# Decoder layer on one core: pair loops written out, and a broadcast by one fp32 matmul split into two fp32r matmuls

## The chip, the core and the metric

The kernel runs on one NeuronCore of one Trainium2 chip. The metric is the device time of one execution in microseconds (us); a kernel's time is the median of its runs. PE is the matmul engine (PEld its weight loads), DVE the vector engine, ACT the scalar engine, POOL GpSimd, SP the queue that issues the DMA transfers. "fp32r" is a four-byte type in which PE multiplies in one pass; an fp32 matmul shows two records in the trace. Wherever the kernel wants more than the precision of fp32r it splits a value into a rounded high part and the low remainder (`_hi`, `_lo`).

## The reference, cut to what matters

```python
x = x + attn(_layernorm(x))      # 32 heads of 128, q and k RMS-normed over all 4096 columns
x = x + xattn(_layernorm(x))     # quantised x @ quantised context
x = x + ffn(_layernorm(x))       # base linear + 8 low-rank experts weighted by a router

# inside attn, x is (2, 256, 512):
q = x @ Wq + bq;  k = x @ Wk + bk;  v = x @ Wv + bv        # each (2, 256, 4096)
k = gk * k * rsqrt(mean(k * k, axis=-1) + 1e-6)             # q likewise
attn = softmax(einsum('bhqd,bhkd->bhqk', q, k) / sqrt(128))
out = einsum('bhqk,bhkd->bhqd', attn, v) ... @ Wo + bo
```

The key norm that the change touches is `rsqrt(mean(k*k))`: one number per token, 512 tokens. Keys lie transposed (a head's 128 columns on the partitions, tokens along the row), so the 512 numbers are needed on every partition.

## The kernel before

All is on one core; each engine has its own program, written out by hand, and semaphores order them. There is no planner.

**k and q stage.** `project` (L540) makes one head's k (then q) for all 512 tokens: 12 matmuls of 128x512, three for each of four chunks of the model width (high by high, low by high, high by low), L549 to L551. "Unit" u counts them: 0 to 31 for k, 32 to 63 for q. ACT casts the weights to `w_hi` (L785) and takes the result out of PSUM (L799, L800: the square), DVE makes `w_lo` (L1205), POOL adds the squares up (L1056, into `acc_k`, then `acc_q`). `project` waits for `w_lo_dve`, so for DVE's L1205 of its own unit; weights and PSUM results have two buffers each. SP loads raw weights four units ahead and waits for the same semaphore.

**The key norm.** In the first four q units PE sums `acc_k` over partitions (L558), DVE scales it (L1282), POOL takes the power -1/2 (`rk_t`, L1064). DVE makes four diagonal matrices, `diag[:, t, :] = ident * rk_t[:, t]` (L1291), and then the weights' low part of q unit 4 (L1205). PE multiplies a matrix of ones by `diag` (L582), which puts every token's factor on all partitions; DVE copies it to `rkb` (L1294) and works the 32 heads of `k_all` through L1210 (a scalar_tensor_tensor of three operands in SBUF), spread over the q units that follow. On PE the L582 matmul stands between q unit 3 and q unit 4.

**Pair stage.** 16 pairs of heads, four slots each (head by batch). In a slot PE does, for successive slots, `scores`, four transposes of the probabilities (L612), 12 matmuls for v of the next pair, six of the output projection and six of probabilities by v. ACT, DVE and POOL have a `pair` of their own with the slot's casts, softmax and low parts. Pair 0 is written out, pairs 1 to 10 are a hardware loop of five turns (`Fori`, two pairs each), pairs 11 to 14 are written out, pair 15 has its own code. SP's `pair_loads` has a loop for pairs 1 to 7. Inside a loop the numbers that a semaphore is waited for depend on the turn and come from registers.

**Tail.** Cross attention, router and FFN follow, straight code on all engines.

Of the kernel before, what the change touches and what calls it, by code (L numbers as in the profile page):

```python
# [19 lines left out]
F32 = mybir.dt.float32  # L20
# [7 lines left out]
P = 128  # L28
B, S, D = 2, 256, 512
T = B * S  # L30
NT = T // P
# [18 lines left out]
def decoder_layer(nc, x, ctx_t, wk, wq, wv, wo, bk, bq, bv, bo, gk, gq, qscal, ra_w, base_b, router_b, bm_w,  # L50
                  expert_map, out):
    st = ExitStack()
    with st:
        def sem(name):
            return st.enter_context(nc.semaphore(name))
# [18 lines left out]
        def here(name, shape, dt, at=None):  # L74
            return place(name, shape, dt, at)[0]
# [21 lines left out]
        ident = here("ident", [P, P], F32)  # L97
        ident_r = here("ident_r", [P, P], F32R)
        ones = here("ones", [P, P], F32)
        bk_c = here("bk_c", [P, NH], F32)  # L100
        bq_c = here("bq_c", [P, NH], F32)
        bv_c = here("bv_c", [P, NH], F32)
# [20 lines left out]
        acc_k = here("acc_k", [P, T], F32, vh_at + half)  # L123
        acc_q = here("acc_q", [P, T], F32, vh_at + half + 2048)
        rkb = here("rkb", [P, T], F32, vl_at + half)
        diag = here("diag", [P, NT, P], F32, vl_at + half + 2048)
        square = here("square", [P, 2, T], F32, pt_at)

        xin = here("xin", [P, NT, D], F32, q_at + (NH - NT) * T * 4)
# [88 lines left out]
        ssq_out = sem("ssq_out")  # L218
        rms_done = sem("rms_done")
        diag_made = sem("diag_made")  # L220
        rkb_ready = sem("rkb_ready")
        k_normed = sem("k_normed")
        kq_hi = sem("kq_hi")
# [112 lines left out]
        @block.sync  # L336
        def _(sp):
            for t in range(NT):
                sp.dma_start(xin[:, t, :], x[t]).then_inc(x_landed[t], 16)
            for r in range(4):  # L340
                sp.dma_start(raw[:, r, :], wk[r]).then_inc(w_landed[r], 16)
            for dst, src in ((bk_c, bk), (bq_c, bq), (bv_c, bv), (g_c, gk), (gq_c, gq)):
                sp.dma_start(dst[:], src).then_inc(const_landed, 16)

            def load_heads(w, i, before):

                for r in range(4):
                    sp.wait_ge(w_lo_dve, before + 4 * i + r - 3)
                    sp.dma_start(raw[:, r, :], w[bass.ds(4 * i + r, 1)].rearrange("a p n -> (a p) n")
                                 ).then_inc(w_landed[r], 16)  # L350

            sp.dma_start(qs_b[:], qscal.partition_broadcast(P)).then_inc(qs_landed, 16)
            for i in range(1, NH // 4):
                load_heads(wk, i, 0)
                if i <= NT:
                    g = slice(2 * (i - 1), 2 * i)
                    sp.dma_start(ctx_f[:, g, :], ctx_t[:, g, :]).then_inc(ctx_landed[i - 1], 16)
                if i == NT:
                    sp.dma_start(bo_b[:], bo.partition_broadcast(P)).then_inc(x_bo_landed, 16)
                    for t in range(NT):  # L360
                        sp.dma_start(xb[:, t, :], x[t]).then_inc(x_bo_landed, 16)
            sp.wait_ge(ctx_quantised, B * NC // 2)
            sp.dma_start(ctx_kept, ctx_k[:]).then_inc(ctx_kept_out, 16)
            with sp.Fori(0, NH // 4) as i:
                load_heads(wq, i, NH)

            def load_wv(pair, c, n):
                sp.dma_start(raw[:, n, :], wv[bass.ds(2 * pair + c, 1)].rearrange("a p n -> (a p) n")
                             ).then_inc(w_landed[n], 16)

            def load_wo(h):
                sp.dma_start(raw[:, 1, :], wo[bass.ds(h, 1)].rearrange("a p n -> (a p) n")
                             ).then_inc(w_landed[1], 16)

            for n in range(4):

                sp.wait_ge(w_lo_dve, U1 - 3 + n if n < 2 else U1 + n - 1)
                load_wv(n // 2, n % 2, n % 2)

            def pair_loads(p):  # L380
                for j in range(3 if peeled(p, NP - 1, NP) else 4):
                    if peeled(p, 0, 1) and j < 2:
                        sp.wait_ge(w_lo_dve, U1 + 3 + j)
                    else:
                        sp.wait_ge(w_lo_pool, 4 * p + j - 1 + peeled(p, NP - 1, NP) * (j // 2))
                    if j % 2:
                        load_wo(2 * p + j // 2)
                    else:
                        load_wv(p + 2, j // 2, 0)

            pair_loads(0)
            with sp.Fori(1, 8) as p:
                pair_loads(p)

            pair_loads(8)
            pair_loads(9)
            sp.wait_ge(scores_ready, 2 * 18)
            pair_loads(10)
            sp.dma_start(wo_last_f[:], wo[NH - 1]).then_inc(wo_last_landed, 16)
            sp.dma_start(ra_f[:], ra_w).then_inc(ra_landed, 16)  # L400
            sp.dma_start(bm_f[:], bm_w).then_inc(bm_landed, 16)
            sp.dma_start(bb_b[:], base_b.partition_broadcast(P)).then_inc(base_b_landed, 16)
            sp.dma_start(rb_b[:], router_b.partition_broadcast(P)).then_inc(router_b_landed, 16)
            sp.dma_start(em_i[:], expert_map.partition_broadcast(P)).then_inc(map_landed, 16)
            pair_loads(11)
            sp.wait_ge(scores_ready, 2 * 22)
            sp.wait_ge(ctx_kept_out, 16)
            sp.dma_start(ctx_q[:], ctx_kept).then_inc(ctx_back, 16)
            for p in range(12, NP - 1):
                pair_loads(p)  # L410
            pair_loads(NP - 1)
            for n, (t, cols, y) in enumerate(out_parts()):
                sp.wait_ge(out_done, n + 1)
                sp.dma_start(out[t][:, cols], xn[:, t, cols]).then_inc(stored, 16)
            sp.wait_ge(stored, 16 * (NT + 1))
# [89 lines left out]
        def _(pe):  # L505
# [62 lines left out]
            for r in range(4):  # L568
                pe.wait_ge(xb_lo_done, r + 1)
                for part in (xb_hi, xb_lo):  # L570
# [7 lines left out]
            sum_squares(acc_k, p_flat[0], NH)  # L578
            project(0, 2, NH)
            project(0, 3, NH)  # L580
            pe.wait_ge(diag_made, NT)
            pe.matmul(p_flat[1], ones[:], diag[:].rearrange("p t n -> p (t n)"), start=True, stop=True  # L582
                      ).then_inc(rkb_ready, 1)
            with pe.Fori(1, NH // 4) as i:
                for r in range(4):
# [90 lines left out]
            def pair(p, par, first=False):  # L676

                for j in range(4):
                    b = j % 2
                    h = 2 * p + j // 2  # L680
                    s = 2 * h + b
                    scores(h + b, 1 - b)
                    transpose_probs(s, b)
                    if first:
                        v_tile(p + 1, j, 1 - par, w_lo_dve, U1 + 4)
                    elif peeled(s, NS - 5, NS - 4):
                        v_tile(p + 1, j, 1 - par, w_lo_pool, 4 * p - 1, range(0, NC - 1))
                    else:
                        v_tile(p + 1, j, 1 - par, w_lo_pool, 4 * p - 1)
                    if not (first and j < 2):  # L690
                        project_out(h - 1, b)
                    if j == 0:
                        pe.wait_ge(v_lo_done, 2 * p + 2)
                    probs_v(s, j // 2, b, par, b)
# [29 lines left out]
            v_tile(0, 3, 0, w_lo_dve, U1 + 2)  # L724
            pe.wait_ge(ssq_out, 2)
            pair(0, 0, first=True)
            with pe.Fori(0, (NP - 6) // 2) as i:
                pair(2 * i + 1, 1)
                pair(2 * i + 2, 0)
            for p in range(NP - 5, NP - 1):  # L730
                pair(p, p % 2)
            last_pair()
# [45 lines left out]
        def _(act):  # L778
# [24 lines left out]

            act.wait_ge(consts_made, 1)
            act.copy(ident_r[:], ident[:])

            def normalise_x(t):
                act.wait_ge(ln_shift, t // 2 + 1)
# [155 lines left out]
                last_out_hi(3)  # L964

            pair(0, 0)
            with act.Fori(0, (NP - 6) // 2) as i:
                pair(2 * i + 1, 1)
                pair(2 * i + 2, 0)
            for p in range(NP - 5, NP - 1):  # L970
                pair(p, p % 2)
            last_pair()
# [63 lines left out]
        def _(pool):  # L1036
# [61 lines left out]
            def pair(p, par):  # L1098
                for j in range(4):
                    h = 2 * p + j // 2  # L1100
                    if j % 2 == 0:
                        split_kq_lo(h + 1)
                        pair_chunk_lo(par, j // 2, 0, 4 + 4 * p + j)
                    else:
                        chunk_lo(wo_lo[:], wo_hi[:], 1, 4 + 4 * p + j)
                    if peeled(p, NP - 5, NP - 4) and j == 0:
                        pool.memset(ones_b[:], 1.0).then_inc(ones_b_made, 1)
# [5 lines left out]
                pair_chunk_lo(1, 1, 0, n + 2)  # L1113

            pair(0, 0)
            with pool.Fori(0, (NP - 6) // 2) as i:
                pair(2 * i + 1, 1)
                pair(2 * i + 2, 0)
            for p in range(NP - 5, NP - 1):
                pair(p, p % 2)  # L1120
            last_pair()
# [17 lines left out]
        def _(dve):  # L1139
# [148 lines left out]
            weights_lo(0, 3, NH)  # L1288
            dve.wait_ge(rms_done, 1)
            for t in range(NT):  # L1290
                dve.tensor_scalar(diag[:, t, :], ident[:], rk_t[:, t:t + 1], None, ALU.mult).then_inc(diag_made, 1)  # L1291
            weights_lo(1, 0, NH)
            dve.wait_ge(rkb_ready, 1)
            link(dve.tensor_copy(rkb[:], p_flat[1]))  # L1294
# [102 lines left out]
                        late_lo((s - 49) // 2)  # L1397

            pair(0, 0)
            with dve.Fori(0, (NP - 6) // 2) as i:  # L1400
                pair(2 * i + 1, 1)
                pair(2 * i + 2, 0)

            for p in range(NP - 5, NP - 1):
                pair(p, p % 2)
# [237 lines left out]
```

## Time and profile before

| | |
|---|---|
| time, median of 3 runs | 532.8 us (531.97 to 533.22) |
| the profiled execution's own time | 531.9 us |
| its span (first to last instruction) | 530.1 us |
| PE busy | 519.8 us, 98% |
| DVE, ACT, POOL busy | 333.8, 355.2, 264.3 us |
| granted TensorE clock | 1.00 |
| k and q stage, about | 9 to 186 us |
| pair stage, about | 186 to 495 us |

The span is what the trace covers; 1.8 us of the profiled time lie around it. Matmul records overlap each other (a 128x512 fp32r matmul shows 0.39 us, but its successor starts 0.23 us after it), so places in PE's stream are read from starts.

### The profile page before, as it was taken

Reading aid. Unit: us, or ns where it says so; the run is one execution under the profiler, and the core shown is the slowest. Engines: PE = TensorE matmul, PEld = TensorE weight load, DVE = VectorE, ACT = ScalarE, POOL = GpSimd, SP = SyncE. Lnnn points to the kernel's source line nnn. Section 1 sums busy time; section 2 is a strip of 40 time slices with the busy share of each in tenths; the row PEclk is TensorE's granted clock in tenths of the full one; section 3 lists DMA queues with packets and bytes.
Section 4 is the critical chain, followed back from the end, with each engine's and each line's share of the span. In section 5 each row is a group of like instructions: output and inputs, shape, how many; then the busy total and the mean of one; then the engine's idle time right before and its main releaser. Section 6 shows DMA issues by size and latency. Waiting matters only on the chain.

```text
span 530.1 us, 9769 instructions
## 1 busy us (share of the span) xinstructions
PE 519.8 (98%) x3203; PEld 461.7 (87%) x3205; DVE 333.8 (63%) x705; ACT 355.2 (67%) x747; POOL 264.3 (50%) x223
## 2 busy tenths in 40 slices
PE   7999999999999999999999999999999999999897
PEld 7888888878888889999999999999999999997586
DVE  6354444276666677666666666666676677767875
ACT  4666666556666767777777677776776777776650
POOL 2344444365554446464655646556465655643350
PEclk9999999999999999999999999999999999999999
DMA  6444634323333221221111221111233412111002
GB/s 184 140 139 153 223 96 162 98 81 99 86 98 95 77 82 41 59 61 61 59 43 56 59 59 59 57 46 54 59 100 103 131 49 61 61 59 41 1 1 80
DMA packets 23495, 43.43 MB, mean 82 GB/s; under 512 B 3632, under 2 KB 3888, under 8 KB 23216
## 3 DMA queue, kind: packets, MB, share of 16 engines
q1 hardware_dynamic: 23472, 43.13, 27.1%
q8 instruction: 13, 0.21, 0.2%
q14 instruction: 10, 0.08, 0.0%
HBM read 41.03 MB, written 2.10 MB: 81 GB/s over the span
## 4 chain that ended last, share of the span: by engine, by line
PE 91%; DVE 4%; ACT 2%; POOL 1%; DMA 0%; issue 0%; POOLq 0%; DVEq 0%; ACTq 0%
PE p_v L628 5%; PE p_o L551 5%; PE p_v L626 5%; PE p_o L549 5%; PE p_o L550 5%; PE p_v L627 5%; PE p_t L549 5%; PE p_t L551 5%; PE p_t L550 5%; PE acc L640 5%; PE acc L641 5%; PE acc L642 5%; PE p_t L612 5%; PE p_o L671 3%; PE p_o L673 3%; PE p_o L672 3%
## 5 line engine op out<-in xcount | busy, mean ns | idle before, releaser
L1205 DVE TENSOR_TENSOR w_lo<-raw,w_hi 128x512 fp32r<-128x512 f32 x64 | 44.2, 690 | 77.0 <-ACT w_hi L785 77.0
L1074 POOL TENSOR_TENSOR wo_lo<-raw,wo_hi 128x512 fp32r<-128x512 f32 x31 | 40.2, 1296 | 100.6 <-ACT wo_hi L939 97.2
L861 ACT ACTIVATE probs<-p_s,nbias,rq_t 128x256 f32<-128x256 f32 x128 | 71.2, 561 | 19.4 <-DVE nbias L1307 19.4
L785 ACT CAST w_hi<-raw 128x512 fp32r<-128x512 f32 x64 | 39.9, 623 | 63.6 <-PE p_t L551 30.3
L626 PE MATMUL p_v<-w_hi,xnt_hi 128*128 128x256 f32 x256 | 77.2, 302 | 0.0
L628 PE MATMUL p_v<-w_hi,xnt_lo 128*128 128x256 f32 x256 | 72.4, 283 | 0.0
L627 PE MATMUL p_v<-w_lo,xnt_hi 128*128 128x256 f32 x256 | 72.3, 282 | 0.0
L1056 POOL TENSOR_TENSOR acc_k<-acc_k,square 128x512 f32<-128x512 f32 x32 | 41.6, 1300 | 53.4 <-ACT square L800 53.4
L1056 POOL TENSOR_TENSOR acc_q<-acc_q,square 128x512 f32<-128x512 f32 x32 | 43.6, 1361 | 40.2 <-ACT square L800 39.9
L915 ACT CAST pt_hi<-p_t 128x512 fp32r<-128x512 f32 x64 | 37.4, 584 | 37.6 <-PE p_t L612 37.6
L1074 POOL TENSOR_TENSOR w_lo<-raw,w_hi 128x512 fp32r<-128x512 f32 x32 | 44.8, 1400 | 23.3 <-ACT w_hi L845 23.3
L1305 DVE TENSOR_REDUCE nmax<-p_s 128x2 f32<-128x512 f32 x64 | 43.9, 686 | 13.4 <-PE p_s L605 12.5
L549 PE MATMUL p_o<-xnt_hi,w_hi 128*128 128x512 f32 x128 | 49.8, 389 | 0.0
L551 PE MATMUL p_o<-xnt_lo,w_hi 128*128 128x512 f32 x128 | 49.8, 389 | 0.0
L550 PE MATMUL p_o<-xnt_hi,w_lo 128*128 128x512 f32 x128 | 49.8, 389 | 0.0
L626 PEld LDWEIGHTS p_v<-w_hi,xnt_hi 128*128 128x128 f32 x256 | 48.9, 191 | 0.3 <-issue 0.2
L627 PEld LDWEIGHTS p_v<-w_lo,xnt_hi 128*128 128x128 f32 x256 | 48.9, 191 | 0.0
L549 PE MATMUL p_t<-xnt_hi,w_hi 128*128 128x512 f32 x124 | 48.8, 393 | 0.0
L628 PEld LDWEIGHTS p_v<-w_hi,xnt_lo 128*128 128x128 f32 x256 | 48.7, 190 | 0.0
L551 PE MATMUL p_t<-xnt_lo,w_hi 128*128 128x512 f32 x124 | 48.3, 389 | 0.0
L550 PE MATMUL p_t<-xnt_hi,w_lo 128*128 128x512 f32 x124 | 48.3, 389 | 0.0
L640 PE MATMUL acc<-wo_hi,o_hi 128*128 128x512 f32 x120 | 47.6, 397 | 0.1
(288 smaller groups left out, 1482.2 us busy)
## 6 DMA issues: line engine op xcount, KB each, us to landing
raw<-in_wv SPq DMA_DIRECT2D x36, 256.0 KB, 2.6
raw<-in_wk SPq DMA_DIRECT2D x32, 256.0 KB, 2.6
raw<-in_wq SPq DMA_DIRECT2D x32, 256.0 KB, 2.6
raw<-in_wo SPq DMA_DIRECT2D x31, 256.0 KB, 2.6
ctx_f<-in_ctx SPq DMA_DIRECT2D x4, 512.0 KB, 3.7
xin<-in_x SPq DMA_DIRECT2D x4, 256.0 KB, 3.1
xb<-in_x SPq DMA_DIRECT2D x4, 256.0 KB, 5.3
ctx_kept<-ctx_k SPq DMA_DIRECT2D x1, 1024.0 KB, 5.1
```

Of the source, the lines that this page charges most:

```text
L549: pe.matmul(p_flat[2 + n], hi[:, c, :], xnt_hi[:, c, :], start=(c == 0), stop=False)
L550: pe.matmul(p_flat[2 + n], lo[:, c, :], xnt_hi[:, c, :], start=False, stop=False)
L551: mm = pe.matmul(p_flat[2 + n], hi[:, c, :], xnt_lo[:, c, :], start=False, stop=(c == NC - 1))
L626: pe.matmul(p_v[:, t % 2, :], xnt_hi[:, c, tt], hi[:, c, :], start=(c == 0), stop=False)
L627: pe.matmul(p_v[:, t % 2, :], xnt_hi[:, c, tt], lo[:, c, :], start=False, stop=False)
L628: mm = pe.matmul(p_v[:, t % 2, :], xnt_lo[:, c, tt], hi[:, c, :], start=False, stop=(c == NC - 1))
L640: pe.matmul(acc[t][:], o_hi[:, tt], wo_hi[:], start=False, stop=False, skip_group_check=True)
L861: act.activation(probs[:, n, a, :], p_s[:, a, :], ACT.Exp, bias=nbias[:, n, a:a + 1], scale=rq_t[:, 2 * b + a:2 * b + a + 1], accum_out=rs ...
L1056: pool.tensor_tensor(sums[:], sums[:], square[:, r % 2, :], ALU.add).then_inc(summed, 1)
L1074: pool.tensor_tensor(dst, raw[:, slot, :], hi, ALU.subtract).then_inc(w_lo_pool, 1)
L1205: dve.tensor_tensor(w_lo[:, n, 0:NC * DH], raw[:, r, :], w_hi[:, n, 0:NC * DH], ALU.subtract).then_inc(w_lo_dve, 1)
L1305: dve.tensor_reduce(nmax[:, n, :], p_s[:], AX.X, ALU.max, negate=True).then_inc(max_done, 1)
```

## The change

Two things. In the pair stage the hardware loops of all five engines are replaced by Python loops: the same instructions in the same order, written out, with constants where registers stood. And the broadcast of the key norms takes a rounded high diagonal and a low diagonal, both fp32r, in two matmuls that add up in PSUM, instead of one fp32 matmul. For that DVE makes four more 128x128 operations (a scalar_tensor_tensor each, `ident * rk_t - diag_hi`), and ACT makes an fp32r copy of the ones at the start.

```diff
-        diag = here("diag", [P, NT, P], F32, vl_at + half + 2048)
+        diag_hi = here("diag_hi", [P, NT, P], F32R, vl_at + half + 2048)
+        diag_lo = here("diag_lo", [P, NT, P], F32R, vh_at)
...
             pair_loads(0)
-            with sp.Fori(1, 8) as p:
+            for p in range(1, 8):
                 pair_loads(p)
...
-            pe.wait_ge(diag_made, NT)
-            pe.matmul(p_flat[1], ones[:], diag[:].rearrange("p t n -> p (t n)"), start=True, stop=True
+            pe.wait_ge(diag_made, 2 * NT)
+            pe.wait_ge(ones_r_made, 1)
+            pe.matmul(p_flat[1], ones_r[:], diag_hi[:].rearrange("p t n -> p (t n)"), start=True, stop=False)
+            pe.matmul(p_flat[1], ones_r[:], diag_lo[:].rearrange("p t n -> p (t n)"), start=False, stop=True
                       ).then_inc(rkb_ready, 1)
...
-            with pe.Fori(0, (NP - 6) // 2) as i:
-                pair(2 * i + 1, 1)
-                pair(2 * i + 2, 0)
+            for p in range(1, NP - 5):
+                pair(p, p % 2)
             for p in range(NP - 5, NP - 1):
                 pair(p, p % 2)
...
             act.wait_ge(consts_made, 1)
             act.copy(ident_r[:], ident[:])
+            act.copy(ones_r[:], ones[:]).then_inc(ones_r_made, 1)
...
             for t in range(NT):
-                dve.tensor_scalar(diag[:, t, :], ident[:], rk_t[:, t:t + 1], None, ALU.mult).then_inc(diag_made, 1)
+                dve.tensor_scalar(diag_hi[:, t, :], ident[:], rk_t[:, t:t + 1], None, ALU.mult).then_inc(diag_made, 1)
+            for t in range(NT):
+                dve.wait_ge(diag_made, NT)
+                dve.scalar_tensor_tensor(out=diag_lo[:, t, :], in0=ident[:], scalar=rk_t[:, t:t + 1],
+                                         in1=diag_hi[:, t, :], op0=ALU.mult, op1=ALU.subtract).then_inc(diag_made, 1)
             weights_lo(1, 0, NH)
             dve.wait_ge(rkb_ready, 1)
             link(dve.tensor_copy(rkb[:], p_flat[1]))
```

The loops of ACT, POOL and DVE change as PE's does.

**DVE, first q units.** On DVE the place is that of the key norm; `w_lo` behind the diagonals is q unit 4's. Before:

```order
L1282 TENSOR_SCALAR ssq<-p_v 128x4 [waits ssq_ready]
L1205 TENSOR_TENSOR w_lo<-raw,w_hi 128x512 [waits w_hi_done]
L1291 TENSOR_SCALAR diag<-ident,rk_t 128x128 [waits rms_done]
L1291 TENSOR_SCALAR diag<-ident,rk_t 128x128 x3
L1205 TENSOR_TENSOR w_lo<-raw,w_hi 128x512 [waits w_hi_done]
L1294 COPY rkb<-p_s 128x512 [waits rkb_ready]
```

The same place on DVE in the changed kernel, whose lines have other numbers:

```order
L1285 TENSOR_SCALAR ssq<-p_v 128x4 [waits ssq_ready]
L1208 TENSOR_TENSOR w_lo<-raw,w_hi 128x512 [waits w_hi_done]
L1294 TENSOR_SCALAR diag_hi<-ident,rk_t 128x128 [waits rms_done]
L1294 TENSOR_SCALAR diag_hi<-ident,rk_t 128x128 x3
L1297 SCALAR_TENSOR_TENSOR diag_lo<-ident,rk_t,diag_hi 128x128 [waits diag_made] x4
L1208 TENSOR_TENSOR w_lo<-raw,w_hi 128x512 [waits w_hi_done]
L1301 COPY rkb<-p_s 128x512 [waits rkb_ready]
```

Four operations, which wait for the four high diagonals of the same engine, now stand ahead of the `w_lo` of q unit 4.

**PE, first q units.** On PE the broadcast stands between q unit 3 (to `p_o`) and the loop of the q units from 4 on, whose first matmul waits for `w_lo_dve`. Before:

```order
L549 MATMUL p_o<-xnt_hi,w_hi 128x512
L550 MATMUL p_o<-xnt_hi,w_lo 128x512
L551 MATMUL p_o<-xnt_lo,w_hi 128x512
L582 MATMUL p_s<-diag,ones 128x512 [waits diag_made]
L584 UNCONDITIONAL_BRANCH
L584 ISA
L546 REGISTER_ALU [waits w_lo_dve]
```

The same place on PE in the changed kernel:

```order
L552 MATMUL p_o<-xnt_hi,w_hi 128x512
L553 MATMUL p_o<-xnt_hi,w_lo 128x512
L554 MATMUL p_o<-xnt_lo,w_hi 128x512
L586 MATMUL p_s<-diag_hi,ones_r 128x512 [waits ones_r_made,diag_made]
L587 MATMUL p_s<-diag_lo,ones_r 128x512
L589 UNCONDITIONAL_BRANCH
L589 ISA
L549 REGISTER_ALU [waits w_lo_dve]
```

One instruction became two, and the first of them waits for all eight diagonals.

**PE, end of the pair loop.** On PE a turn of the loop ends with the probabilities by v and a branch; behind it stands pair 11, or the next turn. Before:

```order
L671 MATMUL p_o<-pt_hi,v_hi 128x256
L672 MATMUL p_o<-pt_hi,v_lo 128x256
L673 MATMUL p_o<-pt_lo,v_hi 128x256
L727 REGISTER_ALU
L727 COMPARE_AND_BRANCH
L603 MATMUL p_s<-k_hi,q_hi 128x256 [waits exp_done]
L604 MATMUL p_s<-k_hi,q_lo 128x256
```

Between two pairs of the changed kernel, on PE:

```order
L676 MATMUL p_o<-pt_hi,v_hi 128x256
L677 MATMUL p_o<-pt_hi,v_lo 128x256
L678 MATMUL p_o<-pt_lo,v_hi 128x256
L608 MATMUL p_s<-k_hi,q_hi 128x256 [waits exp_done,kq_lo]
L609 MATMUL p_s<-k_hi,q_lo 128x256
L610 MATMUL p_s<-k_lo,q_hi 128x256
```

The register instruction and the branch are gone; the matmuls and their order are the same.

## Rows read from the trace of the kernel before

**Rows 1.** The page, parts 1 and 2: busy times and granted clock.

```profile
PE 519.8 (98%) x3203; PEld 461.7 (87%) x3205; DVE 333.8 (63%) x705; ACT 355.2 (67%) x747; POOL 264.3 (50%) x223
PEclk9999999999999999999999999999999999999999
```

**Rows 2.** PE's longest wait: total us, times, longest us.

```profile
PE p_v L511 <- POOL ident L1044: 2.6, 1, 2.6
```

**Rows 3.** Timeline of PE around the broadcast: start, us, instruction.

```profile
111.17 0.39 PE L551 MATMUL p_o<-xnt_lo,w_hi 128*128 128x512 f32 x1
111.40 1.02 PE L582 MATMUL p_s<-diag,ones 128*128 128x512 f32 x2
111.85 0.80 PE L549 MATMUL p_t<-xnt_hi,w_hi 128*128 128x512 f32 x1
112.49 0.40 PE L550 MATMUL p_t<-xnt_hi,w_lo 128*128 128x512 f32 x1
```

**Rows 4.** Timeline of DVE at the diagonals and behind them.

```profile
107.66 1.31 DVE L1291 TENSOR_SCALAR diag<-ident,rk_t 128x128 f32<-128x128 f32 x1 [0.92 <-POOL rk_t L1064]
109.09 1.52 DVE L1291 TENSOR_SCALAR diag<-ident,rk_t 128x128 f32<-128x128 f32 x2
110.33 0.28 DVE L1291 TENSOR_SCALAR diag<-ident,rk_t 128x128 f32<-128x128 f32 x1
110.53 0.68 DVE L1205 TENSOR_TENSOR w_lo<-raw,w_hi 128x512 fp32r<-128x512 f32 x1
112.45 0.69 DVE L1294 COPY rkb<-p_s 128x512 f32<-128x512 f32 x1 [1.24 <-PE p_s L582]
113.18 0.69 DVE L1205 TENSOR_TENSOR w_lo<-raw,w_hi 128x512 fp32r<-128x512 f32 x1
113.79 1.78 DVE L1210 SCALAR_TENSOR_TENSOR k_all<-k_all,g_c,rkb 128x512 f32<-128x512 f32 x1
121.93 2.45 DVE L1210 SCALAR_TENSOR_TENSOR k_all<-k_all,g_c,rkb 128x512 f32<-128x512 f32 x2
```

**Rows 5.** Timeline of POOL over the same stretch.

```profile
107.60 1.29 POOL L1056 TENSOR_TENSOR acc_q<-acc_q,square 128x512 f32<-128x512 f32 x1
109.03 1.30 POOL L1056 TENSOR_TENSOR acc_q<-acc_q,square 128x512 f32<-128x512 f32 x1
110.74 1.61 POOL L1056 TENSOR_TENSOR acc_q<-acc_q,square 128x512 f32<-128x512 f32 x1 [0.41 <-ACT square L800]
113.46 1.56 POOL L1056 TENSOR_TENSOR acc_q<-acc_q,square 128x512 f32<-128x512 f32 x1 [1.11 <-ACT square L800]
122.53 1.30 POOL L1056 TENSOR_TENSOR acc_q<-acc_q,square 128x512 f32<-128x512 f32 x1 [1.42 <-ACT square L800]
```

**Rows 6.** Two DVE lines: ns of one (minimum/median/maximum), first and last start.

```profile
L1210 DVE SCALAR_TENSOR_TENSOR k_all<-k_all,g_c,rkb x32: 740/745/1857, 113.8 to 184.5; 128x512 f32<-128x512 f32 x32
L1262 DVE CAST xb_hi<-xb x4: 420/420/424, 63.9 to 88.4; 128x512 fp32r<-128x512 f32 x4
```

**Rows 7.** Timeline of DVE and PE where PE waits for DVE (486.6 to 487.8 us).

```profile
486.69 0.47 DVE L1356 SCALAR_TENSOR_TENSOR o_last_lo<-p_o,bv_c,o_last_hi 128x256 fp32r<-128x256 f32 x1
487.22 0.50 PE L658 MATMUL acc<-wo_last_hi,o_last_hi 128*128 128x512 f32 x1 [0.33 <-DVE o_last_lo L1356]
487.55 0.39 PE L659 MATMUL acc<-wo_last_hi,o_last_lo 128*128 128x512 f32 x1
```

**Rows 8.** Windows of loop and straight code: us, busy (instructions) PE, PEld, DVE, ACT, POOL.

```profile
214.86:402.61 187.75, 187.75 (x1363) 176.96 (x1361) 125.32 (x280) 136.31 (x321) 104.80 (x81) 1.00 0.21 62
402.61:458.91 56.30, 56.30 (x411) 52.94 (x409) 39.58 (x88) 42.17 (x102) 31.76 (x26) 1.00 0.25 76
```

**Rows 9.** Instruction queue, 402.61 to 475 us: packets, MB, share.

```profile
q8 instruction: 4, 0.07, 0.4%
```

**Rows 10.** Timeline of ACT at the start.

```profile
2.60 0.30 ACT L805 CAST ident_r<-ident 128x128 fp32r<-128x128 f32 x1 [0.59 <-POOL ident L1044]
5.93 0.81 ACT L809 ACTIVATE xin<-xin,x_bias,rstd 128x512 f32<-128x512 f32 x1 [3.03 <-DVE x_bias L1174]
```

More of the change, by code:

```diff
@@ L99, in decoder_layer @@
         ones = here("ones", [P, P], F32)
+        ones_r = here("ones_r", [P, P], F32R)
         bk_c = here("bk_c", [P, NH], F32)
@@ L220, in decoder_layer @@
         diag_made = sem("diag_made")
+        ones_r_made = sem("ones_r_made")
         rkb_ready = sem("rkb_ready")
@@ L966, in _ @@
             pair(0, 0)
-            with act.Fori(0, (NP - 6) // 2) as i:
-                pair(2 * i + 1, 1)
-                pair(2 * i + 2, 0)
+            for p in range(1, NP - 5):
+                pair(p, p % 2)
             for p in range(NP - 5, NP - 1):
@@ L1115, in _ @@
             pair(0, 0)
-            with pool.Fori(0, (NP - 6) // 2) as i:
-                pair(2 * i + 1, 1)
-                pair(2 * i + 2, 0)
+            for p in range(1, NP - 5):
+                pair(p, p % 2)
             for p in range(NP - 5, NP - 1):
@@ L1399, in _ @@
             pair(0, 0)
-            with dve.Fori(0, (NP - 6) // 2) as i:
-                pair(2 * i + 1, 1)
-                pair(2 * i + 2, 0)
+            for p in range(1, NP - 5):
+                pair(p, p % 2)
             for p in range(NP - 5, NP - 1):
```

## The prediction

> **What bounds the kernel now.** I read the page first: PE is busy 98% of the span at the full granted clock, the other engines 50 to 67% [rows 1]. Busy PE is not always PE as the bound, so next come the waits of PE: the longest is 2.6 us, once, at the very start [rows 2]. Then the windows of the pair stage: in 187.75 us of the loop and in 56.30 us behind it PE has no idle time at all [rows 8]. So from the q stage to the last pair PE goes from matmul to matmul; time that PE loses there comes back as time at the end, and time that it saves is saved. A faster or slower ACT, DVE or POOL changes nothing until PE waits for it. So only two questions count: how PE's own work changes, and whether the change makes PE wait. I look at one place for the diagonals and at one stage for the loops.
>
> **The broadcast on PE.** Before, the last matmul of q unit 3 starts at 111.17, its successor's place is 111.40, and the second matmul of q unit 4 starts at 112.49 [rows 3]. A 128x512 fp32r matmul takes 0.23 of PE (111.17 to 111.40), so the first of unit 4 has its place at 112.49 - 0.23 = 112.26, and the fp32 matmul cost 112.26 - 111.40 = 0.86 us. Two fp32r matmuls of the same width cost 2 x 0.23 = 0.46. Alone, that is a gain of **0.40 us**.
>
> **The four low diagonals on DVE.** They stand ahead of `w_lo` of q unit 4, for which PE waits. Before, that `w_lo` ended at 110.53 + 0.68 = 111.21 [rows 4], so DVE had about one microsecond in hand against 112.26. The new operations must fit into it, less the 0.40 that PE arrives earlier.
>
> How long is one? No scalar_tensor_tensor of 128x128 is in the trace. With 512 columns it takes 0.745 [rows 6], with 256 columns 0.47 [rows 7]; the step of 256 columns is 0.27, so 128 columns come to 0.47 - 0.135, about 0.35 (estimate). The bounds are 0.28, the 128x128 tensor_scalar [rows 4], and 0.47, the 128x256 one. The next operation of DVE starts 0.08 before the end of the one before it (110.33 + 0.28 = 110.61 against 110.53), so four queued ones would take 3 x 0.27 + 0.35 = 1.16 us.
>
> But they are not alone. The rows show that DVE and POOL block each other here. The first diagonal took 1.31 instead of 0.28: it ended at 108.97, 0.08 behind the end of POOL's addition, 107.60 + 1.29 = 108.89; the third waited in the same way for the addition of 109.03 [rows 4, 5]. The scalar_tensor_tensor at 113.79 took 1.78 instead of 0.75 and ended at 115.57, behind POOL's 113.46 + 1.56 = 115.02. So a blocked DVE operation works as if started 0.20 before POOL's end (108.97 - 0.28 = 108.69; 115.57 - 0.75 = 114.82). The other way round, POOL's addition of 110.74 took 1.61 instead of 1.30 and ended at 112.35, 1.14 behind the `w_lo` that DVE was in (111.21); the one of 113.46 ended 1.15 behind a `w_lo` (113.87). And POOL gets in between two queued DVE operations: at 113.46 it arrived during a `w_lo` and went ahead of the scalar_tensor_tensor that stood next; at 122.53 it arrived during the first of two scalar_tensor_tensors, and the pair took 2.45 instead of 0.66 + 0.75 = 1.41.
>
> The Trainium skill has this as a rule (SBUF — State Buffer, "SBUF: two separate sides"): VectorE and GpSimd share a pair of ports under an exclusive lock, taken too by a VectorE operation with two SBUF inputs, and whoever starts first blocks the other for the whole instruction. The trace agrees, with 1.78 us where 0.75 is usual. If an operation with two SBUF inputs did not take that lock, the sum would be near that of the first rival below; with it, the one that follows here.
>
> The new operations have two inputs in SBUF, as L1210 has. Step by step:
> - The fourth high diagonal ends at 110.61 as before. DVE's wait for its own semaphore costs 0.04 (112.45 + 0.69 = 113.14 to 113.18, the `w_lo` behind the copy [rows 4]), so the first low diagonal runs 110.65 to 111.00.
> - POOL's third addition arrives at 110.74, since ACT's square does not move. It gets in behind the first low diagonal and ends 1.14 later, at 112.14.
> - The second works as from 112.14 - 0.20 and ends at 112.29, the third at 112.56, the fourth at 112.83. POOL's next addition comes at 113.46, too late to disturb.
> - `w_lo` of unit 4 starts at 112.75 and ends at 113.44.
> - PE reacts to DVE in 0.16: DVE's 486.69 + 0.47 = 487.16, the second matmul behind it at 487.55, so the first one's place was 487.32 [rows 7]. The two broadcast matmuls take 112.99 to 113.45. Unit 4 waits for `w_lo`: its place is 113.44 + 0.16 = 113.60, against 112.26 before.
>
> That is **+1.34 us** with the gain of 0.40 already in it: PE, the bound, stands still for over 1.3 us, first for the diagonals and then for `w_lo`. With the bounds of 0.28 and 0.47 for one operation the same steps give +1.06 and +1.82.
>
> What stands behind it: on DVE the copy to `rkb` and the next `w_lo`, which begin about one microsecond later, but PE needs the latter a unit (12 x 0.23 = 2.8) after 113.60, and it ends near 115; the 32 L1210 have to be done only at the pair stage. SP's next raw load waits for the same `w_lo`, but its slot is read four units, some 11 us, later. POOL ends its third addition no later than before. So one stall, and it isn't given back, for PE has no idle time behind it to take it up.
>
> **The ones in fp32r.** ACT's copy at the start is like that of L805, 0.30, and lies in 3.03 us of idle time ahead of L809 [rows 10]: nothing. Without that cover it would cost 0.30.
>
> **The loops written out.** 40 slots of the loop take 187.75, 4.694 each; 12 straight ones 56.30, 4.692 each [rows 8]. The matmuls are the same. So register instructions and back edges cost PE 0.002 per slot, 0.09 in all; the saving lies between 0 and 0.09, and I take **-0.05**. On the other engines the saved register work is idle time (DVE is busy 125.32 of 187.75). Straight code has to be fetched: in 402.61 to 475 us the larger instruction queue brought four packets, 0.07 MB [rows 9], in a stage where PE is never idle; at that pace 187.75 us need ten. They should cost as little. The bound above is one wait as long as PE's longest, 2.6 [rows 2]; I keep that end for the last rival.
>
> **Sum.** 1.34 - 0.05 = +1.29: the profiled execution's 531.9 becomes 533.2. That execution lies 0.9 below the median of the runs, 532.8, and the forecast is for the median: 532.8 + 1.3 = **534.1 us**. A change of 0.2% (1.07 us) is about what a measurement of this kernel can tell from none.
>
> **The rivals.**
> - *POOL doesn't get in between* (on the other side). If the four low diagonals kept POOL out as one block, they would end at 111.81, `w_lo` at 112.42, and unit 4 would start at 112.58: +0.32, with the loops +0.27, 533.1, no measurable change. It decides at 110.74: POOL must lose against a second operation already queued. For it: the second diagonal did slip in ahead of POOL's addition of 109.03, but before POOL had asked for it. Against it: the two cases above, at 113.46 and 122.53. Chance 0.10.
> - *The high diagonals no longer block.* If writing fp32r took the tensor_scalar out of the mode in which POOL blocks it, the eight operations would start at 107.66 and be done near 111.0; PE would not wait, and only the gain of 0.40 would be left: 532.4. Against it: a cast to fp32r of 128x512 takes 0.42 [rows 6], far below the 0.69 of the copy from PSUM [rows 4], so fp32r runs in the quick mode too. Chance 0.05.
> - *The back edges cost more than the windows show*, on engines that PE follows at the loop's ends. Each of the four taken back edges would have to hide some 0.6 us to make the kernel over 1 us faster in all: about 531.7. PE's windows leave no room for it [rows 8]. Chance 0.05. The Trainium skill speaks for it (Runtime: NRT & Kernel Launch, "Instruction fetch mechanics"): a taken branch out of the prefetched window makes the sequencer fetch again, so full unrolling is to be preferred. No idle time of PE at a back edge is to be seen here.
> - *Fetching the straight code makes PE wait* somewhere, by up to 2.6: 535 to 536.7. Against it stands the straight code of pairs 11 to 14, without idle time of PE. Chance 0.04.
>
> **How the numbers follow.** The forecast's case has 0.76. With its bounds (+1.06 to +1.82, less 0.05) it spans 533.8 to 534.6 on the median. The range for all reaches down to the second rival, 532.4, and up to 534.6 with half a microsecond for the runs' own spread (531.97 to 533.22 before): 532.4 to 535.2. *Slower by over 0.2%*: the forecast's case lies just beyond the bound, so two thirds of it, 0.52, and the last rival: 0.56. *Faster*: the third rival and a little of the second: 0.07. The rest, 0.37, within 0.2%.
>
> **What would show it.** In the changed trace: two broadcast matmuls 0.23 apart; DVE's second low diagonal at over 1 us where the others take 0.35, beside a POOL addition that ends near 112.1; PE idle for some 1.3 us between q units 3 and 4, put down to DVE; no other new wait of PE; pair slots of 4.69. I am wrong if the low diagonals run without a break, if PE starts unit 4 before 112.6, or if pairs 1 to 10 take other than 187.7 us.

## The result, and the profile after

The changed kernel takes 533.26 us (median of 12 runs, 532.46 to 535.09). The kernel before, run beside it, takes 531.92 (median of 12 runs, 531.73 to 533.22). The ratio is 1.0020 with a 95% interval of 1.0012 to 1.0028, which is 0.6 to 1.5 us slower; it is not the quotient of the two medians, which is 1.0025 (+1.34 us). The profiled execution took 533.38 with a span of 531.6.

The waits of PE in the changed kernel (total us, times, longest us) have one new row near the top, which e7 repeats, beside the old first one [rows 2]:

```profile
PE p_v L514 <- POOL ident L1048: 2.6, 1, 2.6
PE p_s L586 <- DVE diag_lo L1297: 1.3, 1, 1.3
```

A wait of 0.4 at the start, for ACT's `xin`, is new as well, but it comes and goes with the execution: the kernel before, profiled once more (e0), has it with 1.3.

The timeline of PE at the broadcast, which answers to [rows 3]:

```profile
111.14 0.39 PE L554 MATMUL p_o<-xnt_lo,w_hi 128*128 128x512 f32 x1
112.84 0.50 PE L586 MATMUL p_s<-diag_hi,ones_r 128*128 128x512 f32 x1 [1.30 <-DVE diag_lo L1297]
113.17 0.40 PE L587 MATMUL p_s<-diag_lo,ones_r 128*128 128x512 f32 x1
113.52 0.49 PE L552 MATMUL p_t<-xnt_hi,w_hi 128*128 128x512 f32 x1
113.85 0.40 PE L553 MATMUL p_t<-xnt_hi,w_lo 128*128 128x512 f32 x1
```

The second matmul of q unit 4 now starts at 113.85 where it started at 112.49. The sums of the squares, which stand two units ahead of the broadcast on PE, began 0.02 earlier (104.98 against 105.00); counted from them, unit 4 is 1.38 us late. Their rows, in the kernel before and in the changed one:

```profile
105.00 0.95 PE L558 MATMUL p_v<-ones,acc_k 128*128 128x1 f32 x8
104.98 0.95 PE L561 MATMUL p_v<-ones,acc_k 128*128 128x1 f32 x8
```

DVE (the four high diagonals first, then the low ones) and POOL over the same stretch, as [rows 4] and [rows 5]:

```profile
107.64 2.94 DVE L1294 TENSOR_SCALAR diag_hi<-ident,rk_t 128x128 fp32r<-128x128 f32 x4 [0.92 <-POOL rk_t L1068]
110.62 0.35 DVE L1297 SCALAR_TENSOR_TENSOR diag_lo<-ident,rk_t,diag_hi 128x128 fp32r<-128x128 f32 x1
110.89 1.63 DVE L1297 SCALAR_TENSOR_TENSOR diag_lo<-ident,rk_t,diag_hi 128x128 fp32r<-128x128 f32 x2
112.70 0.68 DVE L1208 TENSOR_TENSOR w_lo<-raw,w_hi 128x512 fp32r<-128x512 f32 x1
```

```profile
110.71 1.39 POOL L1060 TENSOR_TENSOR acc_q<-acc_q,square 128x512 f32<-128x512 f32 x1 [0.41 <-ACT square L804]
```

One line on the four low diagonals (ns of one, minimum/median/maximum):

```profile
L1297 DVE SCALAR_TENSOR_TENSOR diag_lo<-ident,rk_t,diag_hi x4: 339/345/1369, 110.6 to 112.4; 128x128 fp32r<-128x128 f32 x4
```

Three take 0.34 to 0.35, the second 1.37. It started at 110.89 and ended at 112.26, just behind POOL's addition (110.71 + 1.39 = 112.10). `w_lo` of unit 4 follows at 112.70 and ends at 113.38.

The windows of the pair stage, pairs 1 to 10 and 11 to 13, answer to [rows 8]:

```profile
216.19:403.79 187.60, 187.60 (x1362) 177.32 (x1361) 125.77 (x280) 136.31 (x321) 104.69 (x81) 1.00 0.21 63
403.79:460.13 56.34, 56.34 (x410) 52.96 (x409) 39.60 (x88) 42.20 (x102) 31.70 (x26) 1.00 0.24 76
```

PE has no idle time in either; the ten pairs that were a loop take 187.60 where they took 187.75. They now have to be fetched. The larger instruction queue (packets, MB, share) shows it, over 216.19 to 403.79 us of the changed kernel and then over the loop of the kernel before, 214.86 to 402.61 us:

```profile
q8 instruction: 11, 0.18, 0.4%
q8 instruction: 2, 0.03, 0.1%
```

### The profile page after: what moved, and what is told of

Same layout as the page of the kernel before. It is cut to its first block, busy times and chain, and to the rows that moved or that the text cites. A ratio compares the mean times of both kernels' runs of the same rounds, so it can differ in the third digit from the quotient of the medians.

```text
span 531.6 us, 9101 instructions
## 1 busy us (share of the span) xinstructions
PE 519.7 (98%) x3205; PEld 461.6 (87%) x3205; DVE 335.9 (63%) x709; ACT 355.5 (67%) x748; POOL 263.6 (50%) x223
## 4 chain that ended last, share of the span: by engine, by line
PE 72%; issue 9%; POOL 8%; DVE 5%; ACT 3%; DMA 1%; POOLq 0%; SPq 0%; ACTq 0%; DVEq 0%
POOL acc_k L1060 7%; PE p_v L631 5%; PE p_v L633 5%; PE p_v L632 5%; PE acc L645 5%; PE acc L646 5%; PE p_t L617 5%; PE acc L647 5%; PE p_o L676 3%; PE p_o L678 3%; PE p_o L677 3%; PE p_s L610 3%; PE p_s L609 3%; PE p_s L608 3%; PE p_o L553 3%
```

## The experiments

The theory was that of the prediction: POOL's addition gets in between the low diagonals, PE waits for them and for the `w_lo` behind them, and that is the whole loss; the loops are worth a tenth of a microsecond. The rivals: the low diagonals are slow for another reason, or straight code costs time, or the low part itself costs PE something. Table of all profiles: start of the sums of the squares (L558 of before), from there to the second matmul of q unit 4 (in e4 and e6 of unit 5, since the broadcast stands behind unit 4 there), pairs 1 to 10, and from pair 14's first transposes to the last pair's. All are differences of starts in the traces, in us.

| kernel | sums start | sums to unit 4 | pairs 1 to 10 | pair 14 to the end of 15 | span | median time, ratio to before |
|---|---|---|---|---|---|---|
| before | 105.00 | 7.49 | 187.75 | 31.19 | 530.1 | 531.92 |
| before again (e0) | 105.04 | 7.48 | 187.71 | 31.11 | 530.0 | one run, 531.9 |
| changed | 104.98 | 8.87 | 187.60 | 31.38 | 531.6 | 533.26, 1.0020 |
| changed again (e7) | 104.58 | 8.88 | 187.60 | 31.18 | 530.9 | one run, 532.69 |
| e1, broadcast only | 104.95 | 8.87 | 187.67 | 31.24 | 531.4 | 533.76, 1.0036 |
| e2, loops only | 104.71 | 7.49 | 187.60 | 31.14 | 529.7 | 532.00, 1.0007 |
| e3, POOL behind the diagonals | 105.01 | 7.85 | 187.60 | 31.31 | 530.5 | 532.26, 1.0005 |
| e4, broadcast later | 104.34 | to unit 5: 9.79 | 187.60 | 31.01 | 528.7 | 531.49, 0.9996 |
| e5, identity in PSUM | 105.12 | 8.04 | 187.60 | 31.15 | 530.6 | 532.47, 1.0014 |
| e6, later, loops kept | 106.20 | to unit 5: 9.80 | 187.63 | 31.15 | 530.7 | 531.52, 0.9993 |

From the sums to unit 5 the kernel before takes 115.25 - 105.00 = 10.25; the second matmul of unit 5 there:

```profile
115.25 0.39 PE L550 MATMUL p_o<-xnt_hi,w_lo 128*128 128x512 f32 x1
```

Beside e1 to e4 the kernel before took 531.78 (28 runs), beside e5 to e7 531.75 (21 runs). e1 has five runs of its own, e2 to e6 eleven each.

**e1: the broadcast alone.** The loops of all five engines are put back, PE's here, the others' likewise.

```diff
-            for p in range(1, NP - 5):
-                pair(p, p % 2)
+            with pe.Fori(0, (NP - 6) // 2) as i:
+                pair(2 * i + 1, 1)
+                pair(2 * i + 2, 0)
```

> The new broadcast with the pair loops kept as loops. Theory (the stall at the broadcast is the whole loss): PE starts q unit 4 some 1.38 us later than in the kernel before, the loop slots stay at 4.694 us, and the time is 1.3 to 1.5 us above before (ratio 1.0025 to 1.0028). Rival (the written-out loops cost time of their own, or the loss is elsewhere): the time is near that of before, within 0.5 us, although the stall is there.

Measured: unit 4 is 1.38 late as in the changed kernel, the wait row of PE is the same 1.3, and the ratio is 1.0036 (1.0022 to 1.0050), +1.2 to +2.7 us, of which the expected 1.3 to 1.5 is the lower part. So the broadcast alone carries the loss. Pairs 1 to 10 took 187.67, a little under 187.75.

**e2: the loops alone.** The loops written out in the kernel before, on all five engines, with the broadcast left in fp32.

```diff
-            with pe.Fori(0, (NP - 6) // 2) as i:
-                pair(2 * i + 1, 1)
-                pair(2 * i + 2, 0)
+            for p in range(1, NP - 5):
+                pair(p, p % 2)
```

> The pair loops written out, with the fp32 broadcast of before. Theory: pairs 1 to 10 take 187.6 us instead of 187.75, nothing else moves, the time is 0.0 to 0.3 us below before. Rival (straight code has to be fetched and costs PE time, in the pair stage or behind it): 0.5 us or more above before, with new idle time of PE.

Measured: pairs 1 to 10 in 187.60, nothing else moved, and PE has no new wait but that for `xin` at the start, which e0 has too; the ratio is 1.0007 (0.9998 to 1.0016). The expected small gain in the trace is there, a gain in the time is not to be seen, and a loss of over 0.9 us is excluded. The window of pairs 1 to 10, as [rows 8], without idle time of PE:

```profile
214.56:402.16 187.60, 187.60 (x1363) 177.31 (x1361) 125.77 (x280) 136.40 (x321) 104.81 (x81) 1.00 0.22 63
```

**e3: POOL behind the diagonals.**

```diff
             for r in range(4):
+                if r == 2:
+                    pool.wait_ge(diag_made, 2 * NT)
                 add_square(0, r, NH, acc_q)
```

> The changed kernel, but POOL's third addition of a q square waits for all eight diagonals, so that it can't stand between the low diagonals. Theory (POOL's addition blocks the second low diagonal for about 1.0 us): the four low diagonals run from 110.62 to 111.78 without a break, q unit 4 starts 0.3 us later than in the kernel before instead of 1.38, and the time is about 1.0 us below the changed kernel, 0.1 to 0.3 above before. Rival (the low diagonals are slow for another reason, such as the wait for their own engine's semaphore): the second one still takes over 1 us, and the time stays 1.3 above before.

Measured: the four run without a break. The timelines of DVE and of POOL:

```profile
110.65 1.14 DVE L1299 SCALAR_TENSOR_TENSOR diag_lo<-ident,rk_t,diag_hi 128x128 fp32r<-128x128 f32 x4
111.70 0.69 DVE L1210 TENSOR_TENSOR w_lo<-raw,w_hi 128x512 fp32r<-128x512 f32 x1
```

```profile
111.87 3.37 POOL L1060 TENSOR_TENSOR acc_q<-acc_q,square 128x512 f32<-128x512 f32 x2 [1.54 <-DVE diag_lo L1299]
```

1.14 us for four against 2.16 in the changed kernel; unit 4 is 0.36 late instead of 1.38, and the ratio is 1.0005 (0.9996 to 1.0014). Nothing but POOL's start was changed, so POOL's addition made one microsecond of the loss. The wait for the engine's own semaphore, still there, did not.

**e4: the broadcast later.** DVE makes unit 4's `w_lo` ahead of the low diagonals, and PE does unit 4 ahead of the broadcast; DVE's loop behind leaves out unit 5's `w_lo`, which now stands ahead of it.

```diff
+            project(1, 0, NH)
             pe.wait_ge(diag_made, 2 * NT)
             pe.wait_ge(ones_r_made, 1)
...
-            with pe.Fori(1, NH // 4) as i:
+            for r in range(1, 4):
+                project(1, r, NH)
+            with pe.Fori(2, NH // 4) as i:
...
+            weights_lo(1, 0, NH)
             for t in range(NT):
                 dve.wait_ge(diag_made, NT)
...
-            weights_lo(1, 0, NH)
+            weights_lo(1, 1, NH)
             dve.wait_ge(rkb_ready, 1)
```

> The changed kernel with the two broadcast matmuls moved behind q unit 4, and with the weights' low part of q unit 4 ahead of the low diagonals on DVE. POOL still blocks a low diagonal, but nobody waits for it. Theory (only the wait costs; the two fp32r matmuls are 0.40 us shorter than the fp32 one): PE has no idle time there, q unit 5 starts 0.40 us earlier than in the kernel before, and with the written-out loops the time is 0.4 to 0.6 us below before, 1.7 to 1.9 below the changed kernel. Rival (the low part costs PE something by itself, such as slower matmuls or a reload): no gain against before.

Measured, in the timelines of DVE and of PE:

```profile
109.87 0.68 DVE L1211 TENSOR_TENSOR w_lo<-raw,w_hi 128x512 fp32r<-128x512 f32 x1
110.47 2.16 DVE L1301 SCALAR_TENSOR_TENSOR diag_lo<-ident,rk_t,diag_hi 128x128 fp32r<-128x128 f32 x4
```

```profile
113.23 0.39 PE L554 MATMUL p_t<-xnt_lo,w_hi 128*128 128x512 f32 x1
113.45 0.39 PE L587 MATMUL p_s<-diag_hi,ones_r 128*128 128x512 f32 x1
113.68 0.39 PE L588 MATMUL p_s<-diag_lo,ones_r 128*128 128x512 f32 x1
113.91 0.39 PE L552 MATMUL p_o<-xnt_hi,w_hi 128*128 128x512 f32 x1
114.13 0.39 PE L553 MATMUL p_o<-xnt_hi,w_lo 128*128 128x512 f32 x1
```

The low diagonals still take 2.16 us beside POOL, and no one waits for them: PE goes on at 0.22 to 0.23 a matmul. From the sums to unit 5 it takes 9.79 against 10.25, 0.46 less. The two matmuls take 113.91 - 113.45 = 0.46, as worked out, so the low part costs PE nothing beyond its own 0.23, and the fp32 matmul was 0.40 dearer than the two; the other 0.06 lies mostly in unit 4, whose twelve matmuls take 2.72 here (110.73 to 113.45) and took 2.76 behind the fp32 one (112.26 to 115.02). The ratio is 0.9996 (0.9987 to 1.0005): against the changed kernel 533.26 - 531.49 = 1.8 less; against before a gain of 0.3, a little under the expected 0.4 to 0.6, that the runs don't separate from none.

**e5: the identity in PSUM.**

```diff
+            pe.transpose(p_flat[0][:, P:2 * P], ident[:], ident[:])
             sum_squares(acc_k, p_flat[0], NH)
...
-                dve.scalar_tensor_tensor(out=diag_lo[:, t, :], in0=ident[:], scalar=rk_t[:, t:t + 1],
+                dve.scalar_tensor_tensor(out=diag_lo[:, t, :], in0=p_flat[0][:, P:2 * P], scalar=rk_t[:, t:t + 1],
```

> The changed kernel, but the low diagonals read the identity from PSUM, where PE has put it by one more 128x128 transpose ahead of the sums (0.11 us of PE), so that each of them has only one input in SBUF. POOL's additions are not moved. Theory (POOL blocks a DVE operation because it has two inputs in SBUF): the four run unbroken, about 1.15 us in all, while POOL's third addition runs beside them in 1.29 us and is not lengthened; then the weights' low part, which has two inputs in SBUF, is blocked for 0.1 us at most; q unit 4 starts 0.4 to 0.5 us later than in the kernel before, and the time is about 0.9 us below the changed kernel. Rival (any DVE operation waits while POOL works): the second one still takes 1.3 us or more and the time stays 1.3 us above before.

Measured, in the timelines of DVE and of POOL:

```profile
110.76 1.13 DVE L1298 SCALAR_TENSOR_TENSOR diag_lo<-p_v,rk_t,diag_hi 128x128 fp32r<-128x128 f32 x4
111.80 0.88 DVE L1209 TENSOR_TENSOR w_lo<-raw,w_hi 128x512 fp32r<-128x512 f32 x1
```

```profile
110.85 1.28 POOL L1061 TENSOR_TENSOR acc_q<-acc_q,square 128x512 f32<-128x512 f32 x1 [0.41 <-ACT square L805]
```

The same four operations run unbroken right beside POOL's addition, and it isn't lengthened either. The `w_lo` behind them, both inputs in SBUF, is blocked for 0.2. It is the place of the inputs that decides. The Trainium skill states that a VectorE instruction with two inputs in SBUF contends with a GpSimd instruction that reads SBUF, and that one with at most one such input, outside its two-port modes, does not (SBUF — State Buffer, "SBUF: two separate sides"). The trace agrees, with one operand moved: 1.37 us against 0.34 for the second low diagonal. Counted from the sums, unit 4 is 0.55 late, a little more than expected; the added transpose ahead of the sums takes 0.12 more. The ratio is 1.0014 (1.0005 to 1.0023).

**e6: later, with the loops kept.** The edit of e4 with the loops of e1.

> The broadcast moved behind q unit 4 as in the run e4, with the pair loops kept as loops. Theory (the loops are worth 0.1 us): the same as e4 within 0.3 us, 0.2 to 0.5 us below before. Rival (written-out loops cost a few tenths outside the profiled stretch, as the ratio of the run with the loops alone, 1.0007, may hint): 0.4 us or more below e4.

Measured: from the sums to unit 5 9.80, as in e4, and a time of 531.52 against 531.49 in e4, with the kernel before at 531.75 and 531.78 beside them: the hint of the rival is not borne out. The ratio is 0.9993 (0.9984 to 1.0002). Its profiled execution had a late start, which the waits of DVE show, first in e6, then in e4:

```profile
DVE stats L1170 <- DMA xin<-in_x: 4.7, 2, 3.5
```

```profile
DVE stats L1167 <- DMA xin<-in_x: 3.4, 1, 3.4
```

DVE waits 1.3 longer for the first transfers, and the sums start at 106.20 instead of 104.34; where the rest of the 1.86 comes from was not followed. The start is the place where these profiles differ most.

**e7 and e0: both kernels again.**

> The changed kernel once more, for its profile. If the 0.2 us that the last pair took longer in its first profile belong to the change, they are there again; if they are a matter of the execution, the last pair takes 31.2 us from the start of pair 14's transposes to its last, as in the kernel before, or something else between 31.0 and 31.4. The stall at the broadcast is there again with 1.38 us in all.

> The kernel before once more, for its profile: how much its stages differ from one execution to the next. Expected: the q stage and the loop of pairs the same within 0.1 us, the start (to the sums of the squares) and the last pair different by some tenths.

Measured: the stall is there again, 8.88 us from the sums to unit 4 against 7.48. The last pairs took 31.18 this time, so the 0.2 of the first profile belong to the execution and not to the change. The start moved by 0.4 between the two profiles of the changed kernel. Those of the kernel before differ by 0.04 in the start, 0.05 in pairs 1 to 10 and 0.08 in the last pairs, less than expected.

## Why the prediction was right or wrong

**The mechanism was right, and its steps can be ticked off.** One low diagonal takes 0.345 (estimated 0.35); the first starts at 110.62 (110.65), POOL's addition gets in behind it, the second ends at 112.26 (112.29), the fourth at 112.78 (112.83), `w_lo` ends at 113.38 (113.44), unit 4 loses 1.38 (1.34). That the loss agrees to 0.04 is in part luck, for two small misses offset each other: `w_lo` ended 0.06 sooner than worked out, and PE, counted as in the prediction, took 0.24 from there (113.85 - 0.23 - 113.38) where 0.16 was worked out. e3 and e5 show the cause by freeing the low diagonals from POOL in two ways, e4 that the delay costs only because PE waits. The first rival, four diagonals in one block, is what e3 brought about on purpose, with 0.36 for the 0.32 worked out. The second and third rivals are gone: the four `diag_hi` in fp32r were blocked as before (2.94 in all, against 107.66 to 110.61 = 2.95), and no loop gave half a microsecond.

**The gain of the broadcast.** 0.40 was worked out, and the two matmuls of e4 bear it out (0.46 against 0.86); up to unit 5, e4 and e6 gain 0.46 and 0.45.

**The loops.** Four profiles with loops have 187.75, 187.71, 187.67 and 187.63 for pairs 1 to 10, six without have 187.60: a mean gain of 0.09, at most 0.15 where 0.05 was taken and 0.09 was the upper bound. The bound came from the straight code of pairs 11 to 13, and that runs at 56.34 / 12 = 4.695 a slot in the changed kernel too, slower than 4.690 in pairs 1 to 10. The reason was not looked for. Fetching eleven packets in that stretch showed no idle time of PE, which settles the last rival for the trace. The Trainium skill says that a taken branch to code outside the prefetched window has to wait for a fetch, one reason to prefer full unrolling (Runtime: NRT & Kernel Launch, "Instruction fetch mechanics"). Here the written-out form is ahead by 0.09 us in the trace, for four taken back edges on each of PE, DVE, ACT and POOL; but PE shows no idle time in the loop, and the two instruction queues brought three packets in all over its five turns, so few of the back edges can have led to such a fetch.

**The step that failed** is "the forecast is for the median: 532.8 + 1.3". The change was sized well, +1.29 against +1.34 by the medians (1.1 by the ratio); the base was not. The three runs shown had a median of 532.8, and twelve give 531.92: the profiled execution with its 531.9 lay where most runs lie. The 0.9 that was put on top was the spread of three runs, and the forecast became 534.1, 2.2 above the kernel before as it is, twice the 1.1 of the measured ratio. The same sum on the profiled execution, 531.9 + 1.3 = 533.2, meets 533.26. Two of the four times known then, 531.97 and 531.9, already spoke for the lower base. But a profiled execution is no safe base either: that of e4 lies 0.9 below its median (530.58, 531.49), that of e6 1.0 above (532.52, 531.52). The traces show where such executions differ: the sums started anywhere from 104.34 to 106.20 in ten profiles, while the time from there to the end repeats within 0.3 for the same kernel, most of that in the last pairs. In e6 the first transfers came late; for the other profiles the cause of the spread was not looked for.

**The chances.** Slower by over 0.2% had 0.56 and no change 0.37; the ratio, 1.0020, lies on the line between the two, so the runs don't decide between them. They do exclude a faster kernel, which had 0.07.

**The account of the changed kernel's span**, 531.6 - 530.1 = +1.5 in the first pair of profiles: +1.38 at the broadcast, -0.15 in pairs 1 to 10, +0.19 in the last pairs, which e7 does not repeat, and less than 0.1 elsewhere. What stays open is whether the written-out loops by themselves change the time by a few tenths outside what a profile shows: e2 against before gives +0.07% with an interval that holds zero, the changed kernel against e1 points the other way, and e4 and e6 are equal.

## What to carry to other kernels

Before an operation is put on an engine, look at what stands behind it in that engine's queue and who waits for that: four operations of 0.35 us, put ahead of the one that the bounding engine needs, cost 1.4 us, and the same four behind it, with the broadcast one unit later, cost nothing and let the intended gain of 0.4 through in the trace. Operations of two engines that block each other are to be priced as a chain, where each queued small one can wait for a whole long one of the other engine; an operand in another memory takes it out of the chain. And a change worked out from a trace can be surer than the base that it is added to: here a median of three lay 0.9 from that of twelve, and single profiled executions up to 1.0 from their medians, against a change of 1.3.

## What the runs showed of the hardware

- POOL got between two queued DVE operations with two inputs in SBUF each time it was seen to ask during the first one, with 1.0 us of delay for a 0.34 us operation; with one of the two inputs in PSUM neither engine held up the other (0.34 and 1.28 us side by side, e5).
- A 128x512 fp32 matmul took 0.86 us of PE, worked out from starts, and two fp32r ones 0.46 where PE didn't wait (e4). The granted clock was 1.00 (2.4 GHz) in the stretch of 110.50 to 113.90 us of the changed kernel, with PE's 1.3 us of idle time in it.
- Ten pairs written out, some 1360 matmuls with their loads, took 11 fetched packets on the larger instruction queue instead of two, and 187.60 us instead of 187.63 to 187.75.
